# Products of a fp32r matmul kernel on half arrays of 64 rows instead of whole arrays of 128

## The reference

```python
z1 = einsum('bfi,bir->bfr', x, v) / 512
z  = einsum('bfr,bor->bfo', z1, v) / 16
y  = einsum('bfi,oi->bfo', x, W) + fc_bias + z + cond
out = x + gelu(y)          # exact gelu
```

## Time and profile before

| | before |
|---|---|
| median of 3 runs | 395.2 us (394.72 to 396.36) |
| the profiled execution | 396.18 us, of which 394.4 us from first to last instruction |
| PE busy | 99% of the span, 1673 matmuls |
| PE weight loads, DVE, ACT busy | 80%, 75%, 53% |
| granted TensorE clock | 0.999 of full, the 2.4 GHz level |
| HBM traffic | 176 GB/s over the span |

### The profile page before, as it was taken

One profiled execution on the slowest core, in us unless ns is written; L12 is line 12 of the kernel. 1 busy time (PEld: TensorE's weight loads), 2 busy tenths in 40 slices (PEclk: granted clock), 3 DMA queues, 4 the chain that ended last, 5 costly groups with the idle time before them and its releaser, 6 DMA issues.

```text
span 394.4 us, 4983 instructions
## 1 busy us (share of the span) xinstructions
PE 388.6 (99%) x1673; PEld 315.9 (80%) x1673; DVE 295.9 (75%) x190; ACT 211.0 (53%) x214; POOL 0.7 (0%) x5
## 2 busy tenths in 40 slices
PE   8999999999999999999999999999999999999995
PEld 3678888888888888888888888888888888888884
DVE  4668997777797776797767797677788777788732
ACT  3477465645466545465545555655455645555622
POOL 0000000000000000000000000000000000000000
PEclk9999999999999999999999999999999999999999
DMA  6891895567655567655567655557755557753222
GB/s 187 256 285 55 271 347 183 196 206 239 217 180 169 197 194 239 228 175 177 189 188 239 231 185 165 190 186 239 232 188 168 188 182 239 241 183 110 108 106 106
DMA packets 21800, 77.56 MB, mean 197 GB/s; under 512 B 4352, under 2 KB 4480, under 8 KB 17824
## 3 DMA queue, kind: packets, MB, share of 16 engines
q1 hardware_dynamic: 21136, 76.27, 58.5%
q10 hardware_dynamic: 656, 1.18, 1.0%
HBM read 35.75 MB, written 33.55 MB: 176 GB/s over the span
## 4 chain that ended last, share of the span: by engine, by line
PE 98%; ACT 1%; DVE 0%; POOLq 0%; issue 0%
PE y L388 29%; PE y L396 29%; PE y L392 29%; PE update L444 7%; PE update L429 2%; ACT result L279 1%; PE y L451 1%; DVE result L339 0%; POOLq L51 0%; POOLq L516 0%
## 5 line engine op out<-in xcount | busy, mean ns | idle before, releaser
L388 PE MATMUL y<-x_high,w_high 128*128 128x512 f32 x512 | 197.8, 392 | 0.1
L392 PE MATMUL y<-x_low,w_high 128*128 128x512 f32 x512 | 197.1, 391 | 0.0
L279 ACT ACTIVATE result<-y,bias 128x512 f32<-128x512 f32 x128 | 87.8, 689 | 162.5 <-PE y L396 157.7
L396 PE MATMUL y<-x_high,w_low 128*128 128x512 f32 x512 | 138.7, 391 | 0.0
L298 DVE SCALAR_TENSOR_TENSOR full_w<-update,base_w 128x2048 f32<-128x2048 f32 (+1 forms) x38 | 74.2, 1952 | 79.3 <-PE update L444 74.4
L388 PEld LDWEIGHTS y<-x_high,w_high 128*128 128x128 f32 x512 | 96.5, 189 | 22.9 <-issue 2.4
L396 PEld LDWEIGHTS y<-x_high,w_low 128*128 128x128 f32 x512 | 96.7, 189 | 20.2
L392 PEld LDWEIGHTS y<-x_low,w_high 128*128 128x128 f32 x512 | 96.7, 189 | 20.1
L339 DVE TENSOR_TENSOR result<-result,x_in 128x1024 f32<-128x1024 f32 (+1 forms) x65 | 78.0, 1200 | 10.4 <-ACT result L279 10.4
L294 DVE TENSOR_TENSOR x_low<-x_in,x_high 128x2048 fp32r<-128x2048 f32 (+1 forms) x38 | 74.0, 1946 | 4.2 <-ACT x_high L242 4.2
L294 DVE TENSOR_TENSOR w_low<-full_w,w_high 128x2048 fp32r<-128x2048 f32 (+1 forms) x38 | 74.0, 1947 | 0.5
(11 more groups left out here) (10 smaller groups left out, 6.1 us busy)
## 6 DMA issues: line engine op xcount, KB each, us to landing
out_t<-result SPq DMA_DIRECT2D x63, 512.0 KB, 3.5
x_in<-x_t SPq DMA_DIRECT2D x31, 1024.0 KB, 6.3
f_stack<-f_parts SPq DMA_DIRECT2D x93, 64.0 KB, 5.4
f_stack<-f_parts SPq DMA_DIRECT2D x62, 32.0 KB, 4.7
x_in<-x_t ACTq DMA_DIRECT2D x4, 256.0 KB, 9.5
base_w<-w_t SPq DMA_DIRECT2D x4, 256.0 KB, 8.3
f_parts<-factors SPq DMA_DIRECT2D x1, 896.0 KB, 6.8
out_t<-result SPq DMA_DIRECT2D x2, 256.0 KB, 2.4
```

Of the source, the lines that this page charges most:

```text
L279: nc.scalar.activation(result[j % SLOTS][:, m, :], y[m][:, :], ACT.Gelu, bias=bias[:, bass.ds(b * CHUNKS + m, 1)]).then_inc(gelu_ready, 1)
L388: nc.tensor.matmul(y[m][:, :], w_high[slot][:, c, m * P:(m + 1) * P], x_high[slot][:, c, :], start=(c == 0), stop=False)
L392: nc.tensor.matmul(y[m][:, :], w_high[slot][:, c, m * P:(m + 1) * P], x_low[slot][:, c, :], start=False, stop=False)
L396: mm = nc.tensor.matmul(y[m][:, :], w_low[slot][:, c, m * P:(m + 1) * P], x_high[slot][:, c, :], start=False, stop=(c == CHUNKS - 1))
```

## The change

The products of batches 2 to 30 are cut in two along the contraction: one matmul takes partitions 0 to 63 of a chunk, another 64 to 127. Each of these two halves of the array works on another bank of `y` at a time. A batch is now four phases of 24 half products; `PHASES` says which `m` the lower and the upper half of the array work on. Phase 0 opens `y0` (lower rows) and `y1` (upper rows), phase 1 opens `y2` and `y3`, phase 2 closes `y1` and `y0`, phase 3 closes `y3` and `y2`. The filled part of `f_stack` is written twice, at partitions 0 and 64, so that the four updates are four matmuls of 64 rows, by turns on each half. The zeroing of `f_stack` and its semaphore go away. Batches 0, 1 and 31 keep their products on the whole array.

```diff
-    STACK = 4
-    STACK_DMAS = 5
+    TILES = 2
+    TILE = P // TILES
+    STACK_DMAS = 5 * TILES
+    PHASES = ((0, 1), (2, 3), (1, 0), (3, 2))
...
+                for copy in range(TILES):
+                    row = copy * TILE
+                    for g, sides, pair in ((0, slice(0, 2), high.to_broadcast([RANK, 2, FEATURES])),
...
+                        sp.dma_start(f_stack[slot][row + g * RANK:row + (g + 1) * RANK, sides, :].bitcast(fp32),
+                                     pair).then_inc(stacked[slot], 16)
...
-            sp.wait_ge(stack_zeroed, SLOTS)
...
-                    act.wait_ge(y_ready, CHUNKS * b + m + 1)
+                    act.wait_ge(y_ready, CHUNKS * b + (m if is_whole(t, j) else m // TILES * TILES + 1) + 1)
...
-            for s in range(SLOTS):
-                nc.vector.memset(f_stack[s][STACK * RANK:P, :, :].bitcast(fp32), 0.0).then_inc(stack_zeroed, 1)
...
+            def half_product(w, x, half, m, c, first, last):
+
+                rows = half_rows(half)
+                return nc.tensor.matmul(y[m][:, :], w[rows, c, m * P:(m + 1) * P], x[rows, c, :],
+                                        start=first, stop=last)
+
+            def halves(b, slot, phase):
+
+                tiles = PHASES[phase]
+                opens = phase < CHUNKS // TILES
+                if opens:
+
+                    pe.wait_ge(gelu_ready, CHUNKS * (b - 1) + max(tiles) + 1)
+                else:
+
+                    pe.wait_ge(half_summed, CHUNKS * (b - PIECEWISE) + max(tiles) + 1)
+                for c in range(CHUNKS):
+                    for half, m in enumerate(tiles):
+                        half_product(w_high[slot], x_high[slot], half, m, c, opens and c == 0, False)
+                    for half, m in enumerate(tiles):
+                        half_product(w_high[slot], x_low[slot], half, m, c, False, False)
+                if phase == 0:
+                    pe.wait_ge(w_low_ready, made(b))
+                for c in range(CHUNKS):
+                    for half, m in enumerate(tiles):
+                        mm = half_product(w_low[slot], x_high[slot], half, m, c, False,
+                                          not opens and c == CHUNKS - 1)
+                        if c == CHUNKS - 1:
+                            mm.then_inc(half_summed if opens else y_ready, 1)
...
-                    mm = nc.tensor.matmul(update[:, c, :], f_stack[slot][:, 0, c * P:(c + 1) * P],
-                                          f_stack[slot][:, 1, :], start=True, stop=True)
+                    rows = half_rows(c % TILES)
+                    mm = nc.tensor.matmul(update[:, c, :], f_stack[slot][rows, 0, c * P:(c + 1) * P],
+                                          f_stack[slot][rows, 1, :], start=True, stop=True)
```

More of the change, by code:

```diff
@@ L96, in cond_residual_kernel @@
         idle_zeroed = sem("idle_zeroed")
-        stack_zeroed = sem("stack_zeroed")
         update_ready = sem("update_ready")
@@ L105, in cond_residual_kernel @@
         x_low_ready = sem("x_low_ready")
+        half_summed = sem("half_summed")
         y_ready = sem("y_ready")
@@ L140, in is_last, with is_whole, half_rows @@
             return isinstance(t, int) and t == GROUPS - 1 and j == UNROLL - 1
+        def is_whole(t, j):
+            return piecewise(t, j) or is_last(t, j)
+        def half_rows(half):
+            return slice(half * TILE, (half + 1) * TILE)
         def next_batch(t, j):
@@ L157, in stack_factors @@
                 high, low = parts[:, 0:1, :], parts[:, 1:2, :]
[L158 to L163, removed]
+                for copy in range(TILES):
+                    row = copy * TILE
+                    for g, sides, pair in ((0, slice(0, 2), high.to_broadcast([RANK, 2, FEATURES])),
+                                           (1, slice(0, 2), parts[:, 0:2, :]),
+                                           (2, slice(0, 1), low), (2, slice(1, 2), high),
+                                           (3, slice(0, 2), low.to_broadcast([RANK, 2, FEATURES]))):
+                        sp.dma_start(f_stack[slot][row + g * RANK:row + (g + 1) * RANK, sides, :].bitcast(fp32),
+                                     pair).then_inc(stacked[slot], 16)
             sp.dma_start(f_first[:, :], factors[0:RANK, 0, :]).then_inc(f_first_loaded, 16)
@@ L438, in rank_update @@
                 pe.wait_ge(stacked[slot], 16 * STACK_DMAS * uses)
-                if piecewise(t, j):
-                    pe.wait_ge(stack_zeroed, SLOTS)
                 pe.wait_ge(full_w_ready, made(b - 1))
                 for c in range(CHUNKS):
-                    mm = nc.tensor.matmul(update[:, c, :], f_stack[slot][:, 0, c * P:(c + 1) * P],
-                                          f_stack[slot][:, 1, :], start=True, stop=True)
+                    rows = half_rows(c % TILES)
+                    mm = nc.tensor.matmul(update[:, c, :], f_stack[slot][rows, 0, c * P:(c + 1) * P],
+                                          f_stack[slot][rows, 1, :], start=True, stop=True)
                     if piecewise(t, j) or c == CHUNKS - 1:
@@ L480, in step @@
                 pe.wait_ge(x_low_ready, made(b))
+                if not is_last(t, j):
+                    for phase in range(CHUNKS):
+                        halves(b, slot, phase)
+                    return
                 for m in range(CHUNKS):
```

## The result

The changed kernel takes 398.7 us (median of 4, 398.5 to 400.5) against 395.4 in the same runs: a ratio of 1.0092, 95% interval 1.0076 to 1.0108. It is slower by 0.9%, or 3.3 us. The spans of the profiled executions differ by 2.4 us: 394.4 before, 396.8 after. The time is inside the range forecast (388 to 430), and 2.3 us under the 401 of the likeliest case.

The account below looks back on a forecast made before the run. The prediction took PE, busy 99%, as the bound. Start 4.3, the batches from 3 to 31 0.6 and batch 31 0.6 sum to 5.5 us, on the median 395.2 giving 401 us; range 388 to 430.

Parts of the forecast that it names:

- p stays at 0.2267: On PE, a pair of half matmuls, one on each half of the array, takes 0.2267 us, as one whole matmul does.
- The updates give 0.45 us per batch, PE's work is 11.34: Four update matmuls become two pairs, 0.45 us less per batch; PE's work in a batch is then 11.34 us.
- The ring, 3.88 + 35p = 11.81: Batch time: 3.88 us from phase 2's last pair through Gelu, `w_high`, Gelu to phase 0, plus 35 pairs: 11.81 us.
- `w_low` just fits: `w_low` is done 5.33 us after phase 2's last matmul starts; PE wants its first load of it at 5.36.
- The start, +4.3: Batch 3's products start at 54.4 instead of 49.83, held by a stack: +4.3 us, with 1 and 6 as ends.
- Batch 4's stack is the expensive one: Its tenth DMA lands at 53.9; PE, done with batch 2 at 49.5, stands there for 4.4 us.
- The three halved updates up to batch 2 give 1.35 back: At the start, these updates save 1.35 us, against batch 1's stack landing 0 to 1.6 us late.
- the switches taken as 0: Four switches between whole and half array on PE, below 0.2 us each, counted as 0.
- Batch 31, +0.6: No update in front, so phase 3's 2.7 us hides 3.0 us until `w_high`, and `w_low` comes as late: +0.6 us.
- The gap did not go away: Rival: the other half's work bridges the 0.0134 us idle in each matmul; pairs take 0.214 us, total 388; chance 0.23.
- The halves do not disturb each other: Rival: they do, loads with hand-over setting the pace: 0.24 us per pair, 414 us, or 0.295, 483 us; chance 0.21.
- they do not take turns: Rival: the halves do, at 0.38 us per pair, some 610 us, or 0.453, 705 us; chance 0.10.

## Why the prediction was right

- **p stays at 0.2267.** Right, and it was the step with the widest bounds. Only the picture was off: the ring has the upper half's weights one load later, and both halves start together, within the 0.01 us of the rows.
- **The updates give 0.45 us per batch, PE's work is 11.34.** Right: 11.33 where nothing else binds.
- **The ring, 3.88 + 35p = 11.81.** Right in mechanism and size: the first products of two batches in a row start 11.75 (192.71 to 204.46) and 11.85 us apart (to 216.31), 11.79 over the 27 from 51.28 to 369.59. Two terms were off and cancel, which is luck. ACT starts its Gelu 0.62 us behind the last pair (188.97 to 189.59), not 0.51; and the uncovered load counts once, 0.11, because both halves load at the same time. That gives 3.74 + 0.11 + 7.93 = 11.78. The 27 batches add less than 0.1 us, not 0.6.
- **`w_low` just fits.** Right: it is ready at 194.41, and in the run with `w_high` last, where it is ready 6.02 us behind the start of phase 2's last pair (197.41 to 203.43) instead of 5.44, it was the second wait.
- **The start, +4.3.** Mis-sized, by a wrong step: it is 1.45. The step "Batch 4's stack is the expensive one" failed, and the wait of 3 to 5 us near 50 us did not come. Its DMAs were issued from 40.72, exactly as before, for the result in front of them did not come 1.3 us later; they landed after a median of 4.4 us and not 6.0; and PE arrived 1 us later than I had it. What held PE was batch 3's stack, for which the sum has no term: 1.6 us, up to 39.07. Its landing is slow in both kernels, behind the 3 MB of loads: a median of 8.7 us before and 8.9 now. But before, its 5 DMAs were issued from 19.70 to 22.95; by that median they had landed near 31.7, 5 us ahead of PE. Now its 10 DMAs stand behind 20 others, and the last of them is issued at 30.3 and lands at 39.03. The doubled stack on whole arrays loses as much (1.4 us) and shows that this is the queue and not the halves. That the start costs anything near the forecast is partly luck: the wait that was named is absent, and one that was not named is there.
- **"The three halved updates up to batch 2 give 1.35 back", and the switches taken as 0.** Both are wrong, and for one reason: the updates for batches 1 and 2 stand between whole products. From the one to the other it is 12.16 us (18.96 to 31.12), against 12.18 before. The switch there and back costs 0.40 us, which no row showed.
- **Batch 31, +0.6.** It is 0.8: some 0.2 at its start, which are in the 0.3 above, and 0.6 inside it. Of these 0.3 are the stop for `w_low` (0.54 us from 382.43 to 382.97 instead of 0.23), and most of the rest is the load that is uncovered after each of the two waits.
- **The rivals.** The gap did not go away: it goes with the operands' type. The halves do not disturb each other, with nearly twice the instructions on PE (3065 against 1673), so that neither 0.24 nor 0.295 came; and they do not take turns. One sum among the rivals is off by a little: 50 x 0.38 is 19.0 and not 19.2, about 6 us of the 610.

## What to carry to other kernels

When two accumulations run side by side, both end late: count the work that is left between the first finished result and the next use of its bank, and put into it everything that the draining engine does there, not the draining alone. An operation of an engine that sits idle half the time can still be the bound if it stands in that ring; moving it in front of the wait gave 12 us here, where the change alone lost 3. And a saving by smaller tiles must be weighed against the switch of tile shape around it, which here costs 0.40 of the 0.45 us that it would save. Last, when DMAs are added to a queue, follow every transfer behind them up to its landing: the one that waits need not be the one whose own issue moved most.

## What was not expected of the hardware

- Two half matmuls of 64 rows on the two halves start together and take the time of one whole matmul, 0.2267 us per pair; their two loads overlap as well: after a wait the next pair starts 0.33 us later instead of 0.23 (192.71 to 193.04), so 0.1 us is uncovered, as for one whole matmul.
- From the whole array to halves and back, around two pairs, costs 0.40 us (1.31 for four steps instead of 0.91).
- Matmuls of 512 columns that each have a weight load of their own start 0.2267 us apart in fp32r and 0.216 in bf16, at the same clock. With 512 columns taken as 0.2133 us, as the prediction does, that is 13 ns more and 2 to 3 ns more. Whether it is the change of weights that costs them is not shown: no matmul here goes without one.
